# Routing of a token group moved between the halves of an inverse transform, and GpSimd's small work set between its scatters

## The reference

```
x = x + s4d(layernorm(x))        # long convolution with a kernel K, then (x + y + x*D) normalised, * ln_w + ln_b
x = x + moe(layernorm(x))        # 8 experts, 2 chosen of them, plus one shared expert
x = x + attention(layernorm(x))  # 16 heads of 8, causal, ALiBi
x = x + moe(layernorm(x))        # the same weights again

moe: logits = xf @ gate_w + gate_b;  top_w, top_i = top_k(logits, 2);  gw = softmax(top_w)
     out = sum over e of combine[:, e] * (gelu(xf @ w1[e] + b1[e]) @ w2[e] + b2[e])
     shared = gelu(xf @ ws1 + bs1) @ ws2 + bs2
```

## Time and profile before

| | us |
|---|---|
| median of three runs | 991.98 |
| the profiled execution | 991.34 |
| its span | 989.6 |
| front stage, up to ScalarE's first instruction of the next stage | 266.68 |
| busy: TensorE, VectorE, ScalarE, GpSimd | 672.2, 651.1, 425.6, 469.3 |

### The profile page before, as it was taken

One profiled execution on the slowest core, in us unless ns is written; L12 is line 12 of the kernel. 1 busy time (PEld: TensorE's weight loads), 2 busy tenths in 40 slices (PEclk: granted clock), 3 DMA queues, 4 the chain that ended last, 5 costly groups with the idle time before them and its releaser, 6 DMA issues. The chain is left out here.

```text
span 989.6 us, 21187 instructions
## 1 busy us (share of the span) xinstructions
PE 672.2 (68%) x7378; PEld 488.8 (49%) x7378; DVE 651.1 (66%) x1444; ACT 425.6 (43%) x854; POOL 469.3 (47%) x573
## 2 busy tenths in 40 slices
PE   0369843880099994034898988889884278899970
PEld 0164321660089994022555555555552156789960
DVE  6989973980078884763566676676671097588865
ACT  6541354430055552341455545545543233455543
POOL 2037738687347776360012115515516346277770
PEclk9968975995599998557999999999998599899995
DMA  9310002231155441302112222322311130444417
GB/s 291 90 33 1 0 1 61 63 79 52 36 83 89 93 95 45 146 16 73 53 50 66 64 64 72 85 67 69 86 29 30 30 60 28 62 99 96 96 39 255
DMA packets 137507, 70.45 MB, mean 71 GB/s; under 512 B 89237, under 2 KB 126619, under 8 KB 137400
## 3 DMA queue, kind: packets, MB, share of 16 engines
q1 hardware_dynamic: 113646, 44.16, 19.5%
q0 software_dynamic: 9088, 16.88, 6.0%
q10 hardware_dynamic: 14672, 8.06, 2.9%
HBM read 26.61 MB, written 30.50 MB: 58 GB/s over the span
## 5 line engine op out<-in xcount | busy, mean ns | idle before, releaser
L1985 DVE TENSOR_REDUCE ARENA<-banks 128x2 f32<-128x512 f32 (+1 forms) x192 | 126.8, 688 | 101.6 <-PE banks L1764 99.4
L1508 ACT ACTIVATE ARENA<-banks,ARENA 128x256 f32<-128x256 f32 x312 | 122.1, 475 | 102.2 <-PE banks L1470 86.1
L1468 PE MATMUL banks<-ARENA,W1H 128*128 128x256 f16 x312 | 87.2, 280 | 59.2 <-DMA ARENA<-slots 52.2
L1932 ACT ACTIVATE ARENA<-banks 128x1536 f32<-128x1536 f32 x64 | 91.9, 1437 | 63.4 <-PE banks L1795 63.4
L1482 PE MATMUL banks<-W2L,ARENA 128*128 x624 | 110.6, 220 | 2.7 <-DVE ARENA L1529 2.4
L1483 PE MATMUL banks<-W2H,ARENA 128*128 x624 | 110.1, 219 | 0.1
L1484 PE MATMUL banks<-W2H,ARENA 128*128 x624 | 110.1, 219 | 0.0
L1452 POOL DMA_INDIRECT expert_out_f<-ARENA x78 | 83.1, 1065 | 49.6 <-issue 26.2
L1452 POOL DMA_INDIRECT expert_out_g<-ARENA x78 | 81.4, 1044 | 49.3 <-issue 25.6
L1054 POOL DMA_INDIRECT slots<-ARENA,PLACE x64 | 76.6, 1198 | 43.7 <-issue 23.7
L1550 DVE TENSOR_TENSOR ARENA<-ARENA 128x1024 f16<-128x1024 f32 x78 | 95.6, 1226 | 2.7
(11 more groups left out here) (319 smaller groups left out, 1880.5 us busy)
## 6 DMA issues: line engine op xcount, KB each, us to landing
spread<-ARENA ACTq DMA_DIRECT2D x48, 128.0 KB, 2.0
ARENA<-expert_out_f SPq DMA_DIRECT2D x8, 512.0 KB, 7.1
ARENA<-spread SPq DMA_DIRECT2D x16, 256.0 KB, 2.6
ARENA<-spread SPq DMA_DIRECT2D x64, 64.0 KB, 2.4
ARENA<-expert_out_g SPq DMA_DIRECT2D x8, 512.0 KB, 6.8
XT<-in_w SPq DMA_DIRECT2D x10, 256.0 KB, 7.6
slots<-EMPTY SPq DMA_DIRECT2D x16, 129.0 KB, 4.5
ARENA<-in_w SPq DMA_DIRECT2D x8, 256.0 KB, 6.8
```

The costliest lines, as they stand in the source:

```text
L1468: pe.matmul(out, t.W1H[:, e, ms], XST[i][:, 0], start=True, stop=False)
L1508: ins = nc.scalar.activation(HF[i % 2][:, m], UP[i % 2][:, m], ACT.Gelu, bias=BIAS[i % 4][:, m:m + 1], scale=1.0 / WS)
L1932: nc.scalar.activation(PR[G % 2], t.psum_all[:, 5:8, :], ACT.Exp, scale=1.0 / LOGIT).then_inc(exps, 1)
L1985: dve.tensor_reduce(out, src, AX.X, ALU.max).then_inc(m_red, 1)
```

## The change

On TensorE `inverse` can now be asked for one of its halves. The first half of the last inverse is followed by the transposes and the gate of group 0, then by the second half and the rank of group 0; `up(0)`, `up(1)`, `gate(1)`, `down(0)` and `rank(1)` follow before the loop. On ScalarE the two copies to XT come ahead of `convolved(2)`, and `gelu(0)` ahead of `convolved(3)`, with a wait for all sums. On VectorE `choose(0)` and `order(0)` come up around `norm_offsets(1)` and `scale(2)`, `split_step(0)` comes ahead of `scale(3)`, and `choose(1)` and `order(1)` ahead of the loop. GpSimd loses `finish(3)`: VectorE now adds both halves of the last group. The scatters of group 0 are called in parts, and `finish(2)`, `root(3)`, `root_again(2)` and `root_again(3)` stand between them.

```
@@ finish(g), GpSimd
-                for tt in range(TPB if g < NCG - 1 else 1):
+                for tt in range(TPB):
@@ GpSimd's list
             root_again(1)
+            route.dispatch_first(pool, 0, range(0, 2))
             finish(2)
             root(3)
-            finish(3)
-            pool.wait_ge(rows_set, 1)
-            route.dispatch_first(pool, 0)
+            route.dispatch_first(pool, 0, range(2, 4))
             root_again(2)
+            route.dispatch_first(pool, 0, range(4, GRP))
+            route.dispatch_second(pool, 0, range(0, 1))
             root_again(3)
-            route.dispatch_second(pool, 0)
+            route.dispatch_second(pool, 0, range(1, 2))
@@ ScalarE's list
             normal(0)
-            convolved(2)
             act.wait_ge(job_low, len(jobs))
             for k in range(2):
                 act.wait_ge(halves_mm, k + 1)
                 nc.scalar.activation(t.XT[:, k, 0:GRP * P], ps[k].bitcast(F16), ACT.Copy).then_inc(halves, 1)
+            convolved(2)
             normal(1)
-            convolved(3)
             nc.scalar.activation(t.GATE[0:1, 1:2], t.MHALF[0:1, 0:1], ACT.Gelu).then_inc(primed, 1)
             act.wait_ge(primed, 1)
             act.sem_inc(hidden, MT)
+            act.wait_ge(ys_ready, 2 * NCG)
+            gelu(0)
+            convolved(3)
             normal(2)
-            gelu(0)
+            gelu(1)
             normal(3)
-            for g in range(1, NG):
+            for g in range(2, NG):
                 gelu(g)
@@ TensorE's list
-            inverse(NCG - 1)
+            inverse(NCG - 1, range(0, 1))
             (waits and transposes of group 0)
             gate(0)
+            inverse(NCG - 1, range(1, TPB))
             route.rank(pe, 0, ps[7][:, P:2 * P])
             pe.wait_ge(prod_ready, 2 * NCG)
-            for g in range(NG):
+            up(0)
+            up(1)
+            gate(1)
+            pe.wait_ge(rn_ready, 2 * NCG)
+            down(0)
+            route.rank(pe, 1, ps[7][:, P:2 * P])
+            for g in range(2, NG):
                 group = g // 2 + 1
                 if g % 2 == 1 and group < NGRP:
                     gate(group)
                 up(g)
-                if g == 1:
-                    pe.wait_ge(rn_ready, 2 * NCG)
-                if g >= 1:
-                    down(g - 1)
+                down(g - 1)
@@ residual_statistics(3), VectorE
-                    dve.wait_ge(scaled, 2 * NCG)
                     dve.wait_ge(biased, NCG)
-                    rn = RN[:, 2 * (g % 2) + 1, :].rearrange("p (b h) -> p b h", h=D)
-                    res = t.RES[:, 2 * CB * g + 1:2 * CB * (g + 1):2, :]
-                    link(tt_(res, res, rn, ALU.add))
-                    dve.wait_ge(res_ready, 2 * g + 1)
+                    for tt in range(TPB):
+                        dve.wait_ge(scaled, 2 * g + tt + 1)
+                        rn = RN[:, 2 * (g % 2) + tt, :].rearrange("p (b h) -> p b h", h=D)
+                        res = t.RES[:, 2 * CB * g + tt:2 * CB * (g + 1):2, :]
+                        ins = tt_(res, res, rn, ALU.add)
+                    link(ins)
@@ VectorE's list
             offsets(2)
+            choose(0)
             norm_offsets(1)
             scale(2)
+            order(0)
             statistics(3)
+            row_lows(1)
+            residual_statistics(2)
             offsets(3)
-            choose(0)
-            order(0)
-            residual_statistics(2)
-            row_lows(1)
+            split_step(0)
+            norm_offsets(2)
             scale(3)
             residual_statistics(3)
-            norm_offsets(2)
+            row_lows(2)
+            choose(1)
+            order(1)
             norm_offsets(3)
-            row_lows(2)
-            for g in range(NG):
+            for g in range(1, NG):
@@ dispatch_first, dispatch_second
-    def dispatch_first(pool, g):
+    def dispatch_first(pool, g, tiles=range(GRP)):
-    def dispatch_second(pool, g):
+    def dispatch_second(pool, g, halves=range(2)):
```

More of the change, by code:

```diff
@@ L473, in forward, with inverse @@
                 ins.then_inc(fwd_mm, 1)
-            def inverse(g):
+            def inverse(g, parts=range(TPB)):
                 pe.wait_ge(ys_ready, 2 * g + 2)
-                for tt in range(TPB):
+                for tt in parts:
                     n = 2 * g + tt
@@ L812, in _ @@
             offsets(2)
+            choose(0)
             norm_offsets(1)
             scale(2)
+            order(0)
             statistics(3)
+            row_lows(1)
+            residual_statistics(2)
             offsets(3)
-            choose(0)
-            order(0)
-            residual_statistics(2)
-            row_lows(1)
+            split_step(0)
+            norm_offsets(2)
             scale(3)
             residual_statistics(3)
-            norm_offsets(2)
+            row_lows(2)
+            choose(1)
+            order(1)
             norm_offsets(3)
-            row_lows(2)
-            for g in range(NG):
+            for g in range(1, NG):
                 group = g // 2 + 1
-                if g % 2 == 1 and group < NGRP:
+                if g % 2 == 1 and g > 1 and group < NGRP:
                     choose(group)
                 split_step(g)
-                if g == 0:
+                if g == 1:
                     row_lows(3)
-                if g >= 1:
-                    merge_step(g - 1)
-                if g % 2 == 1 and group < NGRP:
+                merge_step(g - 1)
+                if g % 2 == 1 and g > 1 and group < NGRP:
                     order(group)
@@ L1052, in dispatch_first @@
         pool.wait_ge(iotas, 1 + 2 * done)
-        for i in range(GRP * g, GRP * g + GRP):
+        for i in range(GRP * g + tiles.start, GRP * g + tiles.stop):
             nc.gpsimd.indirect_dma_start(xs, bass.IndirectOffsetOnAxis(ap=t.PLACE[:, 0, i:i + 1], axis=0),
                                          ROWI[:, i, :], None).then_inc(sent[i % GRP // (GRP // 2)], 16)
-    def dispatch_second(pool, g):
+    def dispatch_second(pool, g, halves=range(2)):
         done = g - part.first
-        for h in range(2):
+        for h in halves:
             first = GRP * g + GRP // 2 * h
```

## The result

| | before | after |
|---|---|---|
| median, us | 991.56 (4 runs, 990.97 to 992.01) | 980.6 (4 runs, 978.2 to 985.43) |
| ratio to before | | 0.9896 (95%: 0.9858 to 0.9934) |
| profiled execution, its span | 991.34, 989.6 | 980.27, 978.5 |
| ScalarE's first instruction of the second stage | 266.68 | 255.09 |

The changed kernel is 11 us faster; forecast were 8.8, and the time lies in the range. In a second comparison it had a median of 979.25 and a ratio of 0.9892 (0.9874 to 0.9911), so the gain is not the luck of one run.

What follows compares the result with a forecast made beforehand. GpSimd's own work bounds the first stage: idle 12.4 us less, 1.6 of work gone, stalls about 5 more make a gain of 9, forecast 8.8, so 983.2 us from the median 991.98; range 977.5 to 988.5.

Steps and rivals of the forecast that it cites:

- The bound: End of the first stage: GpSimd's end sets it, and the next stage begins 8.2 us after its last scatter.
- Group 0 comes earlier: Front stage: group 0 is routed before the second half inverse; GpSimd's first scatter at 137.8 us instead of 150.42.
- The half inverse: TensorE, second half of the last inverse: keeps its 5.40 us; the high clock would save 1.7 us.
- GpSimd's list: GpSimd after its wait: scatters, additions and powers in order from 137.8 us, the second scatters ending at 174.7.
- the four first scatters: GpSimd, group 0 after `root_again(2)`: 5.1 us, stretched 2.5 by VectorE's multiplications, additions and `row_lows(2)`, to 159.1.
- The hold of `root_again(2)`: GpSimd: this 1.65 us power stands behind a split's 2.29 us subtraction, from 148.0 to 151.5.
- The ledger: GpSimd's sum: idle 12.4 us less, 1.6 of work gone, stalls and stretched powers up about 5; gain 9.
- the first split's place: VectorE: `split_step(0)` starts near 146.3 us, after the last Gelu near 144.3 and `residual_statistics(2)`.
- Group 1: Routing of group 1: rows set near 141.1, placed at 163.6, 11 us before GpSimd asks at 174.7.
- Rivals 2 and 3: 2: GpSimd waits again, 987 to 989 us, chance 0.17. 3: DMAs hold TensorE at `gate(1)`, slower, chance 0.06.
- The 48 scatters: GpSimd, groups 1 to 3: start at 175.0 instead of 183.84, then keep today's 74.6 us under six splits.
- Rival 1: GpSimd's stalls don't grow, by missed alignment or only casts holding scatters: gain 14, 978.0 us (976.3 with clock); chance 0.17.

Runs made afterwards that it cites:

- `pool_alone`: The kernel before with only GpSimd's new placing of scatters and powers, routing and other engines as before: 989.05 us, ratio 0.9992.
- the subtractions at the end of the stage: The changed kernel with eight more two-input subtractions on VectorE where GpSimd scatters alone: 991.11 us; first scatter of group 1 to last scatter's end 82.92 against 74.66.

## Why the prediction was right

- The bound. GpSimd sets the end of the stage, and the 8.2 us behind it are fixed: 8.22 before and after, 8.15 to 8.32 in the other profiles.
- Group 0 comes earlier. Foreseen 7.7 us from power to first scatter, measured 7.14 (GpSimd's first scatter at 136.73, just outside the 137 to 138.5 that were named as a sign). Counted from the power, the transposes, the copies and the gate lay within 0.2 us of their places; the difference came behind the half inverse, where 1.7 us to the placed rows and 0.7 more to the scatter were given, the 0.7 without a row, and 1.42 and 0.31 measured. The half inverse stayed at the low level of the clock (5.37), as assumed. It ran at the high level in three other kernels, and was worth the 1.7 us given for it in one of them, `pool_alone`; in the other two the slow first half took that back.
- GpSimd's list. The prediction missed by 1.6 us in this part, from 37.2 to 35.56. The step that failed is the four first scatters, "stretched by ... 2.5": they were stretched by 1.0 (5.8 us from the first one's start at 151.00 to the iota at 156.79). The multiplications and additions of VectorE ran there in one piece, 150.92 to 153.42, and met only two scatters; `row_lows(2)` (155.94 to 157.16) met none that it could stretch. Smaller misses cancel in part: the power of `root(3)` was held by `row_lows(1)` (2.59 instead of 1.65 us) and the second scatter behind it took 1.54 us beside the cast of `split_step(0)`, while `finish(2)` was not held, where 0.5 had been given, since there VectorE was the loser (L80, 3.20 us). The list has a slip of 0.2 us as well: 137.8 and 3.0 make 140.8, not 140.6. The hold of `root_again(2)` was foreseen with 3.5 us and came with 3.01.
- The ledger. Idle time fell by 12.6 us (12.4 foreseen) and the moved addition took its 1.6; the term "stalls and stretched powers grow by about 5" was the one mis-sized, at 3.3 measured (scatters of group 0 1.0, powers 2.3). That is where most of the gain beyond the forecast comes from.
- One reason for the first split's place was wrong without harm: the first up-projections ran at the high level (0.22 us a step where 0.43 was assumed), so `gelu(0)` ended near 141.3 and not 144.3; `split_step(0)` stood behind `residual_statistics(2)` and began at 145.64 in either case.
- Group 1. Its rows were set at 143.16, 2 us later than foreseen (VectorE's lost 3.0 us), the DMAs needed 11.5 us to the gate at 154.70; placed at 162.1, 10 us ahead of GpSimd (11 foreseen). Rivals 2 and 3 needed a wait that isn't there.
- The 48 scatters: 74.6 us foreseen, 74.58 measured. GpSimd's groups in this stretch after (they answer to the earlier trace rows), with 59.4 us busy against 59.5:

```profile
L1064 POOL DMA_INDIRECT slots<-ARENA,PLACE x24 | 31.3, 1305 | 7.3 <-issue 7.3
L1077 POOL DMA_INDIRECT slots<-ARENA,PLACE x24 | 28.1, 1170 | 7.2 <-issue 5.5 <-POOL ARENA L1073 1.7
```

- Rival 1 (the stalls don't grow, gain 14) was not far: the gain of 11.1 in GpSimd's sum lies between it and the forecast's 8.8, a little nearer to the forecast, and the first scatter of group 1 at 172.29 lies between the signs of both, 170 and 175. The stalls did grow, by 3.3 us; that two-input and casting work met fewer scatters than assumed was luck in the alignment. Rival 1's other mechanism, that two-input work doesn't hold scatters, is refuted by the subtractions at the end of the stage.

Open: why the two halves of the last inverse exchange clock levels in some runs (a first half of 5.40 to 6.67 us and then a second of 3.68 to 3.71, where most profiles have 3.71 and then 5.37), and what makes the stretch with the attention stage vary by 4 us from run to run. Neither was tried.

## What to carry to other kernels

Where one engine's own work sets the end of a stage, write its timeline as a ledger from the last row that the edit leaves alone: idle times, work, and work that is stretched by another engine. Here that gave the gain to 2 us of 11. Then look at the ledger of the result for the idle time that is left and ask which queued instruction is ready in it: that alone took 2.9 us more off GpSimd's sum. And price VectorE's work beside scatters by its kind (two inputs in SBUF, a cast, or one input), not by its duration: the casts moved to ScalarE, where each is slower, took 5.0 to 5.2 us off that sum.

## What the runs showed of the hardware

- A two-input VectorE instruction of 2.29 us stalls an indirect scatter by up to 1.77 us (1.03 on average back to back), a 2048-wide cast of 1.23 us by 0.7 on average back to back, a one-input reduction of 2.3 us by nothing (74.66 us in either case), and an addition of PSUM to SBUF of 0.69 us by nothing (scatters of 0.96 to 0.98 us beside it).
- An iota of GpSimd, which has no input, took 0.15 us beside those subtractions and 1.17 beside the casts.
- The stall goes both ways: a 128x8 multiplication of 0.16 us took 3.20 us on VectorE behind a scatter and two GpSimd additions.
- Beside casts back to back a scatter took 2.2 us, nearly two casts' length; beside subtractions of 2.29 us back to back it took 2.0, so one passed for each subtraction.
